# mLSTM layer of a four-layer kernel: a half batch's projection, gates and rows in other steps of the pipeline

## The reference, cut to what matters

```python
up = xs @ W_up.T;  x_m, z = up[..., :512], up[..., 512:]
x_conv = conv_b + sum(xp[:, k:k+S, :] * conv_w[:, 0, k] for k in range(4))   # causal, along the tokens
x_act = silu(x_conv)
q, k = blockdiag(x_act, Wq), blockdiag(x_act, Wk);  v = blockdiag(x_m, Wv)
ig, fg = [q, k, v] @ W_i.T + b_i, [q, k, v] @ W_f.T + b_f
lc = cumsum(log_sigmoid(fg))
D = exp(lc_i - lc_j + ig_j - m)  for j <= i, else 0          # m: the row's maximum
C = (q k^T / 8) * D;  h = C v / max(|sum C|, exp(-m))
h = layernorm(h) * norm_w;  h = (h + skip * x_act) * silu(z)
out = x + h @ W_down.T
```

## Time and profile before

| | us |
|---|---|
| median of 3 runs | 3844.08 (3843.38 to 3848.24) |
| the profiled execution, its own time | 3843.91 |
| its span (first to last instruction) | 3842.1 |
| PE busy | 3250.3 (85%) |
| DVE busy | 2155.3 (56%) |
| ACT busy | 2023.2 (53%) |
| POOL busy | 1332.2 (35%) |

### The profile page before, as it was taken

How to read it: one execution, slowest core, us unless ns; L and a number is a source line. 1 busy time by engine, 2 the same in 40 slices (tenths; PEclk the granted TensorE clock), 3 DMA queues, 4 the chain that set the end, 5 groups by cost and what they waited for, 6 DMA issues and landing times. The chain is left out here.

```text
span 3842.1 us, 95200 instructions
## 1 busy us (share of the span) xinstructions
PE 3250.3 (85%) x39424; PEld 1805.6 (47%) x39424; DVE 2155.3 (56%) x4883; ACT 2023.2 (53%) x4339; POOL 1332.2 (35%) x1526
## 2 busy tenths in 40 slices
PE   4999999999965888888888875999993788777887
PEld 2223323332323555555555544677772555555554
DVE  3776777677644565565556543555553455554554
ACT  1665665556544454544544433566652665555565
POOL 2112202221201323324232232222223767776764
PEclk9999999999987899999999988999996899898988
DMA  3000000000011222223222114445443232223322
GB/s 149 1 23 23 1 23 23 23 1 23 12 45 64 73 64 70 62 64 91 60 62 67 45 56 136 137 143 161 141 131 117 61 95 79 87 90 92 100 78 86
DMA packets 265788, 274.44 MB, mean 71 GB/s; under 512 B 23424, under 2 KB 240272, under 8 KB 260496
## 3 DMA queue, kind: packets, MB, share of 16 engines
q1 hardware_dynamic: 260944, 259.50, 22.3%
q10 hardware_dynamic: 4416, 8.86, 0.6%
HBM read 213.96 MB, written 53.81 MB: 70 GB/s over the span
## 5 line engine op out<-in xcount | busy, mean ns | idle before, releaser
L720 DVE TENSOR_TENSOR l_probs<-l_psum,l_decay 128x1024 f32<-128x1024 f32 x512 | 601.8, 1219 | 173.3 <-PE l_psum L602 173.3
L771 ACT ACTIVATE l_sizes<-l_probs 128x2048 f32<-128x2048 f32 x256 | 488.3, 1910 | 279.8 <-DVE l_probs L720 277.0
L1758 ACT ACTIVATE l_logits<-l_logits,l_low 128x100 f32<-128x100 f32 x1024 | 373.6, 368 | 301.4 <-DVE l_low L1738 300.2
L1765 POOL TENSOR_TENSOR l_logits<-l_logits,l_inv 128x400 f32<-128x400 f32 x256 | 224.4, 877 | 625.9 <-DVE l_inv L1744 614.2
L602 PE MATMUL l_psum<-l_qk 32*128 32x512 f32 x2048 | 312.3, 640 | 8.9 <-DVE l_probs L720 8.4
L303 PE MATMUL l_psum<-l_xT,l_w_up 128*128 128x512 f32 x512 | 246.3, 637 | 48.7 <-DVE l_row_var L1391 38.2
L627 PE MATMUL l_psum<-l_sizes,l_ones 128*32 128x512 f32 x2048 | 275.1, 609 | 11.1 <-ACT l_D L775 5.9
L617 PE MATMUL l_psum<-l_probs,l_V 128*32 128x512 f32 x2048 | 269.5, 598 | 7.0 <-DVE l_probs L720 6.2
L1726 PE MATMUL l_psum<-l_PT,l_V_windows 100*32 100x16 f32 x16384 | 197.2, 187 | 53.0 <-DVE l_PT L1750 36.5
L1700 PE MATMUL l_psum<-l_keys,l_q_blocks 128*64 128x100 f32 x4096 | 237.0, 257 | 5.6 <-issue 4.1
L1750 DVE COPY l_PT<-l_psum 100x512 f32<-100x512 f32 x256 | 174.7, 682 | 119.2 <-PE l_psum L1711 119.0
(11 more groups left out here) (258 smaller groups left out, 6278.4 us busy)
## 6 DMA issues: line engine op xcount, KB each, us to landing
l_V_windows<-v_image SPq DMA_DIRECT2D x512, 100.0 KB
l_V_windows<-v_padded SPq DMA_DIRECT2D x512, 100.0 KB
l_E<-rows_c SPq DMA_DIRECT2D x64, 512.0 KB, 6.8
l_xT<-y SPq DMA_DIRECT2D x24, 1024.0 KB, 6.0
y<-l_xT SPq DMA_DIRECT2D x32, 512.0 KB, 3.4
l_e_everywhere<-rows_e SPq DMA_DIRECT2D x112, 128.0 KB, 5.3
l_xT<-x SPq DMA_DIRECT2D x8, 1024.0 KB, 5.0
l_res<-y SPq DMA_DIRECT2D x16, 512.0 KB, 6.3
```

The costliest lines, as they stand in the source:

```text
L720: nc.vector.tensor_tensor(probs[:, N % 3, 2 * p:2 * p + 2, :], ring.region(name).rearrange("p (a n) -> p a n", a=2), decay[:, h:h + 2, s0: ...
L771: nc.scalar.activation(sizes[:, N % 2, :, :], probs[:, N % 3, :, :], ACT.Abs).then_inc(sized, 1)
L1758: nc.scalar.activation(e, e, ACT.Exp, scale=-1.0, bias=self.low[:, N % 4, i:i + 1], accum_out=self.total[:, N % 4, i:i + 1]).then_inc(self ...
L1765: nc.gpsimd.tensor_tensor(p, p, self.inv[:, N % 4, :].unsqueeze(2).to_broadcast([P, STEP, NKEY]), ALU.mult).then_inc(self.p_ready, 1)
```

## The change

The steps of the prepared and finished units are dealt out anew, on all engines alike. Below p = u + 2, n = u + 1, f = u - 1.

| step | fills before | fills now | DVE's extra work before | DVE's extra work now |
|---|---|---|---|---|
| 0 | down(f-1), up(n) | z(f), g(n), gn | residual, convolve(n) | moments, collect; variance behind sums |
| 1 | z(f) | fi(n), q(n) | variance; moments behind sums | rows(n) |
| 2 | g(n), r(f); fi, gn behind sums | r(f), tok(n) | scale; rows, collect, skip behind sums | scale |
| 3 | q(n), tok(n) | up(p), down(f) | none | skip(f), convolve(p), residual(f) |

`down` now waits for the gates one 128-row tile at a time, and goes through its four tiles with both output halves at each. ACT's `up` waits for `skip` tile by tile. POOL does `mask` of the next unit's chunks 0 and 1 in steps 2 and 3, ahead of `gate`; before, behind it. There is one round of steps fewer at the end. Counts and shapes of all instructions stay.

```diff
 
-    n, f = u + 1, u - 1
-    early = {0: [("down", f - 1), ("up", n, 0), ("up", n, 1)], 1: [("z", f, 0), ("z", f, 1)], 2: [("g", n), ("r", f, 0), ("r", f, 1)],
-             3: [("q", n, 0), ("q", n, 1), ("tok", n)]}[t]
-    late = [("fi", n)] if t == 2 else []
-    early, late = ([name for name in names if 0 <= name[1] < UNITS] for names in (early, late))
-    if t == 2 and u % 2 == 0 and u // 2 + 1 < B:
-        late.append(("gn", u // 2 + 1))
-    return early, late
+    p, n, f = u + 2, u + 1, u - 1
+    names = {0: [("z", f, 0), ("z", f, 1), ("g", n)], 1: [("fi", n), ("q", n, 0), ("q", n, 1)], 2: [("r", f, 0), ("r", f, 1), ("tok", n)],
+             3: [("up", p, 0), ("up", p, 1), ("down", f)]}[t]
+    names = [name for name in names if 0 <= name[1] < UNITS]
+    if t == 0 and u % 2 == 0 and u // 2 + 1 < B:
+        names.append(("gn", u // 2 + 1))
+    return names
 
@@
 def layer1_steps():
-    return [(u, t) for u in range(-2, UNITS + 2) for t in range(CHUNKS)]
+    return [(u, t) for u in range(-2, UNITS + 1) for t in range(CHUNKS)]
 
@@
         N = u * CHUNKS + t
-        early, late = layer1_fill(u, t)
-        order += early
+        order += layer1_fill(u, t)
         if 0 <= N <= LAST:
             order.append(("ud", N))
-        order += late
         if 0 <= N + 1 < LAST:
@@
                     if 0 <= n < UNITS:
-                        if t == 2:
+                        if t == 1:
                             sp.wait_ge(c_ready, n + 1)
@@
                             spread_c(4 * n)
+                        if t == 2:
                             spread_c(4 * n + 1)
-                        if t == 3:
-                            spread_c(4 * n + 2)
                             sp.wait_ge(e_ready, n + 1)
@@
                             spread_e(4 * n)
-                    if t == 1 and 0 <= f - 1 < UNITS:
-                        store(f - 1)
+                        if t == 3:
+                            spread_c(4 * n + 2)
+                    if t == 3 and 0 <= f < UNITS:
+                        store(f)
                 for s in range(2):
@@
                     else:
-                        pe.wait_ge(gated, IT * (n + 1))
                         ring.may_fill(pe, name)
-                        for m in range(HALVES):
-                            i = project(nc, ring.region(name)[:, m * BANK:(m + 1) * BANK], wdn, O[n % 2], m, 0, BANK)
+                        for k in range(IT):
+                            pe.wait_ge(gated, IT * n + k + 1)
+                            for m in range(HALVES):
+                                i = nc.tensor.matmul(ring.region(name)[:, m * BANK:(m + 1) * BANK], wdn[:, k, m * P:(m + 1) * P],
+                                                     O[n % 2][:, k, :], start=(k == 0), stop=(k == IT - 1))
                         i.then_inc(ring.filled(name), 1)
@@
                     N = u * CHUNKS + t
-                    early, late = layer1_fill(u, t)
-                    for name in early:
+                    for name in layer1_fill(u, t):
                         fill(name)
@@
                         sums(N)
-                    for name in late:
-                        fill(name)
                     if 0 <= N + 1 < LAST:
@@
                 def variance(f):
+                    ring.is_taken(dve, ("ud", 4 * (f + 1)))
                     dve.wait_ge(n_ready, f + 1)
@@
                 for u, t in layer1_steps():
-                    n, f, N = u + 1, u - 1, u * CHUNKS + t
-                    b = u // 2 + 1 if u % 2 == 0 and u // 2 + 1 < B else None
+                    p, n, f, N = u + 2, u + 1, u - 1, u * CHUNKS + t
+                    b = u // 2 + 1 if t == 0 and u % 2 == 0 and u // 2 + 1 < B else None
                     if 0 <= N < LAST:
@@
                         weigh_queries(N)
-                    if t == 0 and 0 <= f - 1 < UNITS:
-                        residual(f - 1)
-                    if t == 0 and 0 <= n < UNITS:
-                        conv_steps = convolve(n, 0, conv_steps)
-                        conv_steps = convolve(n, 1, conv_steps)
-                    if t == 1 and 0 <= f < UNITS:
-                        variance(f)
+                    if b is not None:
+                        norm.moments(nc, dve, vstep, b)
+                        norm.collect(nc, dve, ring, b)
+                    if t == 1 and 0 <= n < UNITS:
+                        rows(n)
                     if t == 2 and 0 <= f < UNITS:
                         scale(f)
-                    if 0 <= N <= LAST:
-                        sums(N)
-                    if t == 1 and b is not None:
-                        norm.moments(nc, dve, vstep, b)
-                    if t == 2:
-                        if 0 <= n < UNITS:
-                            rows(n)
-                        if b is not None:
-                            norm.collect(nc, dve, ring, b)
+                    if t == 3:
                         if 0 <= f < UNITS:
                             skip(f)
+                        if 0 <= p < UNITS:
+                            conv_steps = convolve(p, 0, conv_steps)
+                            conv_steps = convolve(p, 1, conv_steps)
+                        if 0 <= f < UNITS:
+                            residual(f)
+                    if 0 <= N <= LAST:
+                        sums(N)
+                    if t == 0 and 0 <= f < UNITS:
+                        variance(f)
 
@@
                         ring.is_full(act, ("xv", 4 * (n - 2) + 3))
-                    if n >= 3 and p == 0:
-                        act.wait_ge(skipped, IT * (n - 2))
                     nc.scalar.activation(xm[n % 2][:, 2 * p:2 * p + 2, TAPS - 1:], ring.region(name).rearrange("p (i n) -> p i n", i=2),
@@
                         i = 2 * p + a
+                        if n >= 3:
+                            act.wait_ge(skipped, IT * (n - 3) + i + 1)
                         m = nc.scalar.activation(xa[n % 3][:, i, :], ring.region(name)[:, a * BANK:(a + 1) * BANK], ACT.Identity,
@@
                 def deviation(f):
-                    ring.is_taken(act, ("ud", 4 * (f + 1)))
+                    ring.is_taken(act, ("ud", 4 * f + 3))
                     nc.scalar.activation(NR[f % 2][:, :], NR[f % 2][:, :], ACT.Square, bias=eps[:, :], scale=ROOT_EPS).then_inc(n_ready, 1)
@@
                 for u, t in layer1_steps():
-                    n, f, N = u + 1, u - 1, u * CHUNKS + t
-                    if t < 3 and 0 <= N + 1 < LAST:
+                    p, n, f, N = u + 2, u + 1, u - 1, u * CHUNKS + t
+                    if t < 3 and 0 <= N + 1 < LAST and N >= 0:
                         decay(N + 1)
-                    if t == 0 and 0 <= n < UNITS:
-                        up(n, 0)
-                        up(n, 1)
-                    if t == 1 and (0 <= n < UNITS or 0 <= f < UNITS):
-                        silus(f, n)
-                        nc.scalar.preload_act_table_set(LN_SET)
+                    if t == 0:
+                        if 0 <= n < UNITS or 0 <= f < UNITS:
+                            silus(f, n)
+                            nc.scalar.preload_act_table_set(LN_SET)
+                        if 0 <= n < UNITS:
+                            gates(n)
                         if 0 <= f < UNITS:
                             deviation(f)
-                    if t == 2 and 0 <= n < UNITS:
-                        gates(n)
-                    if t == 3 and 0 <= n < UNITS:
+                    if t == 1 and 0 <= n < UNITS:
+                        log_sigmoid(n)
                         copy_queries(n, 0)
                         copy_queries(n, 1)
+                    if t == 2 and 0 <= n < UNITS:
                         token_values(n)
                         row_exps(n)
-                    if 0 <= N < LAST:
-                        copy_out(N)
-                    if t == 1 and 0 <= f < UNITS:
-                        inverse(f)
-                    if t == 2 and 0 <= n < UNITS:
-                        log_sigmoid(n)
                     if t == 3:
-                        if u % 2 == 0 and u // 2 + 1 < B:
-                            norm.root(nc, act, u // 2 + 1)
+                        if 0 <= p < UNITS:
+                            up(p, 0)
+                            up(p, 1)
                         if 0 <= N + 1 < LAST:
                             decay(N + 1)
+                    if 0 <= N < LAST:
+                        copy_out(N)
+                    if t == 0 and 0 <= f < UNITS:
+                        inverse(f)
+                    if t == 1 and u % 2 == 0 and u // 2 + 1 < B:
+                        norm.root(nc, act, u // 2 + 1)
 
@@
                 for u, t in layer1_steps():
-                    n, f, N = u + 1, u - 1, u * CHUNKS + t
+                    p, n, f, N = u + 2, u + 1, u - 1, u * CHUNKS + t
                     b = u // 2 + 1 if u % 2 == 0 and u // 2 + 1 < B else None
```

(44 more changed lines are left out.)

8 lines of the change are left out of this document (4 added, 4 removed).

## The result

The changed kernel takes **3732.0 us** (median of 4 runs, 3713.4 to 3732.5), the kernel before, run beside it, 3846.2 (4 runs, 3843.4 to 3850.8). That is 114 us less by the medians. The ratio is 0.9695, with a 95% interval from 0.967 to 0.9719, which makes 117 us. The profiled execution took 3732.5 us with a span of 3730.7, 111.4 less than the span before.

What follows compares the result with a forecast made beforehand. PE's 55 us of work was taken as a unit's floor; idle 4.5 and lost clock 2.2 made 61.7, 6.6 less. Over 13 units 86 us, plus 18 at the ends, is 104 off 3844: 3740 us, range 3690 to 3790.

Steps and rivals of the forecast that it cites:

- PE's floor and the clock: Each unit: 55 us of PE work at the upper clock level, plus 2.2 us lost to the lower clock.
- Step 0: PE on `z` and `g`: no idle time, DVE's `moments` being covered by `z`'s 7.0 us.
- Step 1: PE ahead of `sums`, waiting for DVE's `rows` behind ACT's `decay` and three activations: idle 0.7 us a unit.
- Step 2: PE: `r` waits for `weights`, `tok` for `tokens`, 0.3 and 0.2; 0.7 where `row_args` delays `sums`: idle 1.2 us.
- `up`, 0.3: Small waits of PE at the `up` projection in step 3: 0.3 us a unit.
- Step 3: PE before `tokens(N + 1)` waits for DVE's `residual`; DVE 14.9 plus 6.1 from gates and mask, against 18.9: idle 2.3 us.
- The ends: Gain outside the thirteen units: about 7 at `up(1)`, 6 at the last `down`, 5 in light units; 18 us.
- The price of the clock: PE loses 0.5 us to the lower clock for each us of idle; 2.2 us a unit taken.
- the port free: Rival: POOL beside DVE costs nothing and PE is the bound; 58.3 us a unit, 3696 us; chance 0.18.
- The port dearer: Rival: masks also fall on `sums` or `weigh_queries`, step 3 idles 5 us; 64.5 a unit, 3777 us; chance 0.17.
- The round trip: Rival: rows' trip through DRAM delays masks and the gates behind them; 12 us more a unit, 3896 us; chance 0.06.
- No effect: Rival: PE's idle time comes back elsewhere one for one, leaving 3844 us; chance 0.04.

Runs made afterwards that it cites:

- e9: The changed kernel with gates on DVE, step 0's mask after the convolution, fade behind `weigh_queries`, and ACT's `log_sigmoid` ahead of `decay`: 3664.2 us, ratio 0.9518.
- e0: The changed kernel run again unaltered, as base for other runs: 3722.0 us, ratio 0.9677 against the kernel before.
- e5: The changed kernel with POOL's masks of the next unit's chunks 0 and 1 put back behind the gates: 3800.6 us, ratio 0.9886.
- e2: The changed kernel with each gate multiplying only 8 of its 512 columns: 3687.9 us, ratio 0.9589.
- e7: The changed kernel with the gates on DVE and POOL's step 0 mask waiting for the convolution: 3690.1 us, ratio 0.9604; run again, 3698.2.
- e3: The kernel before, with only DVE's convolution moved behind `sums` in step 0: 3886.2 us, ratio 1.0108.
- e1: The changed kernel with POOL's mask of step 0 waiting until the convolution is over: 3699.4 us, ratio 0.9617.

## Why the prediction was right

The forecast was 3740 us, within 3690 to 3790, and 3732 came out. Step by step, with the measured value of the thirteen units in the place of each term:

- **PE's floor and the clock.** 55.0 + 2.2 = 57.2 was forecast, 57.1 measured.
- **Step 0, nothing.** Right in an ordinary unit. The one wait of `z`, 4.45 us, is in the first unit of the stretch and makes 0.3 in the mean of thirteen.
- **Step 1, 0.7.** Measured 10.4 / 13 = 0.8, released by L1354, the old L1357, as said. e9 shows that it is ACT's order ahead of it.
- **Step 2, 1.2.** Too much: only `r` waits, 5.8 / 13 = 0.4. The 0.7 put down for `row_args` holding up `sums` had no row behind it, and named the wrong neighbour: a mask holds `sums` up, and it is `up` that waits.
- **`up`, 0.3.** Too little: 8.1 / 13 = 0.6. What was missed is that a mask of step 2 falls on `sums`, which I gave to the rival only. Two masks land in step 2, and in five units of thirteen the second stretches L1374 to over 2 us. A row of before could have told: the kernel before had the same stretch in every second unit.

```profile
1673.87 2.40 DVE L1377 TENSOR_TENSOR l_faded<-l_state,l_tok_vals 128x264 f32<-128x264 f32 x1 [5.03 <-PE l_psum L1274]
```

- **Step 3, 2.3.** Measured 22.1 / 13 = 1.7, at the place and with the releaser foretold. The port's price, 4 x 1.0 + 2.1 = 6.1, is the measured (4.76 - 2.73) + (12.15 - 8.04) = 6.1. PE's side was 0.8 shorter than my 18.9 in the unit shown (1677.22 to 1695.3, the end of L1215), DVE's also: that unit's last chunk has no `k_gated`, so `weights` to `weigh_queries` take 2.3 instead of 3.0.
- **The sum.** The errors of the steps, 0.8 and 0.6 too much (steps 2 and 3) and 0.3 each too little (`z` and `up`), cancel in part, and so far the closeness of the sum is luck. Idle 4.0 instead of 4.5, a unit 61.1 instead of 61.7, so 92.5 us instead of 86. The ends gave 18.9 instead of 18: 6.0 against 7 for `up(1)`, 4.2 against 6 for the last `down`, and 8.7 left over against 5 for the light units. Only the total of these is firm.
- **The price of the clock**, 0.5 us for each us of idle: 59.4 - 57.1 = 2.3 us for 4.9 us of idle less. But e0, the same kernel with the same waits, had 56.6, so the runs bear this term out only to some 0.5 us a unit.

The Trainium skill ("SBUF — State Buffer", Who interferes with whom) has the two engines' shared port locked by one of them at a time; with whole instructions of POOL lost to DVE, an estimate by that rule is 7.4. The runs give 6.1 here, and in e5 10.4 where the rule makes 4 x 1.27 + 3 x 2.35 = 12.1. The kind of contention is as it says; the price is about a sixth lower on this pair of instructions.

The rivals: **the port free** (3696) fell with the first convolution of 12.15 us; e2 and e7, with nothing or next to nothing of the gates beside DVE, ended near its figure, 3688 and 3690, though neither is that case exactly: e2 kept a mask beside the convolution and e7 gave DVE the gates' own 2.49 us. **The port dearer** (3777) had a true part, `sums` under a mask, but at 0.6 us a unit ahead of `up`, and not 5 in step 3. **The round trip** fell: the gates wait for `skip` (4.64 us in the unit shown), never for a DMA, and e5 was slower without masks ahead of them. **No effect** fell with the result.

The direction of the gain was right for the reason given, that each of the four waits had a piece of DVE's long work ahead of it. But e3 shows that the reason alone is not enough: the same convolution taken from one slot's way and put in another's made the old kernel 41 us slower.

## What to carry to other kernels

Before a long vector instruction group is moved, lay PE's next fills beside it and count the microseconds until the first of them needs a slot, or data, that stands behind the group: here 18 us in step 3, and some 4 in e3. Then count GpSimd's instructions in the same stretch, each at its own price, because they lengthen the group although no semaphore joins the two. An operation whose inputs are ready early (the state's fade) doesn't belong in the short chain that a matmul waits for: moving that one 0.4 us multiply gave 21 to 29 us.

## What the runs showed that I had not expected

- **The price of POOL beside DVE adds up almost exactly.** It is 1.0 us for a gate of 1.27 and 2.1 for a mask of 2.35, so about 0.25 us less than the POOL instruction's own time in each case, whether one mask lies beside the convolution (e1's difference: 2.1), four gates (e2's: 4.1), or four gates and three masks (e5: 10.4). POOL pays too: four gates take 6.65 instead of 5.42 us and a mask 2.80 instead of 2.35. So both sides wait, and it takes both sides' times to see the whole cost.
- **A short instruction waits out the rest of a mask.** L1374 began at 1673.57, 0.3 us into a mask that ended at 1675.60, and went from 0.46 to 2.31 us. That is nearly what a mask adds to the convolution (2.1), but there it lengthens a group of 8 us by a quarter, and here it makes an instruction of half a microsecond five times as long, in a chain that PE's next fill waits for.
- **The clock differs between two executions of one kernel.** Over the same twelve units, the same matmuls kept PE busy for 691.43 us (clock 0.96) in the profile of the changed kernel and 679.30 (0.97) in e0's, and the stretch took 737.17 and 727.45 us. The waits of some 2 us in each unit were there in both. What decides between the two was not tried, and a difference of 10 us between two runs of such a kernel can't be put down to an edit.
